# A two-layer transformer block on one NeuronCore: its feed-forward part computed with hidden units on the partitions, its expert weights loaded tile by tile

## What is computed

```
xn = layernorm(x)
x  = x + distance_attention(xn) + feed_forward(xn)       # layer 0
xn = layernorm(x)
x  = x + attention(xn) + magnitude(xn)                   # layer 1

distance_attention: 16 heads of 8; softmax(-sqrt(max(|q-k|^2, 1e-12))) @ v
feed_forward:  swiglu(h, w1, w2, w3) = (silu(h @ w1.T) * (h @ w3.T)) @ w2.T,  352 hidden units
    shared = swiglu(x, sw1, sw2, sw3)
    each token also goes to the one of 7 experts with the highest sigmoid(x @ router)
    0.5/total * shared + p/total * swiglu(x, expert's weights)
```

## Time and profile before

| | |
|---|---|
| Timed runs | median 1478.41 us (1476.91 to 1479.61, three runs) |
| Profiled execution | span 1475.7 us, first to last instruction; no other time is given for it |
| ACT busy | 1445.4 us, 98% |
| DVE busy | 1245.1 us, 84% |
| PE busy | 1125.2 us, 76%, mean granted clock 0.935 of 2.4 GHz |
| POOL busy | 632.5 us, 43% |
| DMA | 112.73 MB, 76 GB/s in the mean |

### The profile page before, as it was taken

How to read it: one execution, slowest core, us unless ns; L and a number is a source line. 1 busy time by engine, 2 the same in 40 slices (tenths; PEclk the granted TensorE clock), 3 DMA queues, 4 the chain that set the end, 5 groups by cost and what they waited for, 6 DMA issues and landing times.

```text
span 1475.7 us, 21637 instructions
## 1 busy us (share of the span) xinstructions
PE 1125.2 (76%) x7910; PEld 441.5 (30%) x7910; DVE 1245.1 (84%) x2236; ACT 1445.4 (98%) x796; POOL 632.5 (43%) x529
## 2 busy tenths in 40 slices
PE   5587786887887988878878774787778677776766
PEld 2122223144252441542524411232123122221212
DVE  6998887988989879789798787858898898998886
ACT  3999999999999999999999999999999999999998
POOL 5166460754509577595585820732113023022100
PEclk8599998999999999999999997899999999999999
DMA  4843544213242212122121321034033033021020
GB/s 124 247 137 74 160 128 124 58 52 85 79 136 65 56 43 58 38 56 64 31 66 48 84 68 31 20 108 93 28 117 76 31 110 82 27 106 34 22 72 19
DMA packets 104061, 112.73 MB, mean 76 GB/s; under 512 B 41722, under 2 KB 76026, under 8 KB 103946
## 3 DMA queue, kind: packets, MB, share of 16 engines
q1 hardware_dynamic: 98618, 99.47, 24.5%
q0 software_dynamic: 4464, 11.09, 2.7%
q10 hardware_dynamic: 864, 0.69, 0.2%
HBM read 66.52 MB, written 44.70 MB: 75 GB/s over the span
## 4 chain that ended last, share of the span: by engine, by line
ACT 72%; issue 12%; DVE 11%; PE 3%; POOL 2%; DMA 1%; SPq 0%; ACTq 0%; DVEq 0%; POOLq 0%
ACT scores L785 28%; ACT scores L746 25%; ACT exp L1304 11%; DVE exp L1312 5%; DVE scores L695 4%; ACT exp L1300 2%; ACT ht L1037 1%; ACT L785 1%; ACT L746 1%; POOL yro L1091 1%; PE pvb L676 1%; PE ring L661 1%; ACT scores L778 0%; PE ring L1279 0%; POOL at L1254 0%
## 5 line engine op out<-in xcount | busy, mean ns | idle before, releaser
L695 DVE TENSOR_SCALAR scores<-ring 128x1024 f32<-128x1024 f32 x512 | 589.7, 1216 | 28.7 <-PE ring L661 23.5
L785 ACT ACTIVATE scores<-scores 128x8192 f32<-128x8192 f32 x63 | 438.9, 7020 | 0.2
L1304 ACT ACTIVATE exp<-ring 128x1024 f32<-128x1024 f32 x438 | 432.7, 1419 | 0.2
L746 ACT ACTIVATE scores<-scores 128x8192 f32<-128x8192 f32 (+1 forms) x59 | 404.2, 6919 | 0.2
L1279 PE MATMUL ring<-stk 128*128 128x512 bf16 x1024 | 306.7, 385 | 122.8 <-ACT exp L1304 100.1
L676 PE MATMUL pvb<-scores,val 128*9 128x256 f32 x4096 | 324.6, 392 | 80.6 <-issue 38.4
L1312 DVE SCALAR_TENSOR_TENSOR exp<-exp 128x512 f32<-128x512 f32 x438 | 322.6, 758 | 62.2 <-ACT exp L1304 56.3
L661 PE MATMUL ring<-stk 64*128 64x512 bf16 x1024 | 210.4, 408 | 56.6 <-DVE scores L695 44.5
L1279 PEld LDWEIGHTS ring<-stk 128*128 128x128 bf16 x1024 | 65.8, 97 | 338.3 <-ACT exp L1304 234.4
L661 PEld LDWEIGHTS ring<-stk 64*128 64x128 bf16 x1024 | 49.9, 93 | 288.5 <-DVE scores L695 201.8
L676 PEld LDWEIGHTS pvb<-scores,val 128*9 128x9 f32 x4096 | 65.6, 89 | 210.8 <-issue 207.4
(11 more groups left out here) (263 smaller groups left out, 1415.8 us busy)
## 6 DMA issues: line engine op xcount, KB each, us to landing
stk<-stack SPq DMA_DIRECT2D x192, 192.0 KB, 2.8
stack<-qp SPq DMA_DIRECT2D x7, 768.0 KB, 4.7
stack<-kp SPq DMA_DIRECT2D x7, 768.0 KB, 5.7
xj<-xg SPq DMA_DIRECT2D x10, 448.0 KB
yg<-xj POOLq DMA_DIRECT2D x10, 448.0 KB
stack<-qp SPq DMA_DIRECT2D x7, 512.0 KB, 5.1
stack<-kp SPq DMA_DIRECT2D x7, 512.0 KB, 5.1
stk<-sum_rows SPq DMA_DIRECT2D x128, 24.0 KB
```

The costliest lines, as they stand in the source:

```text
L695: nc.vector.tensor_scalar(S[place][:, j * N:(j + 1) * N], tile, 1e-12, None, ALU.max).then_inc(o.release(("qk", group, place, j)), 1)
L746: nc.scalar.activation(part, part, ACT.Sqrt).then_inc(root_done, 1)
L785: nc.scalar.activation(S[place][:], S[place][:], ACT.Exp, scale=-1.0).then_inc(exp_done, 1)
L1304: nc.scalar.activation(EX[k // 2][:, k % 2, :], tile, ACT.Exp, scale=SCALE1).then_inc(o.release(("qk1", n, i)), 1)
```

## The change

The hidden units are put on the partitions from the start: in the up product the weights are now the stationary operand and the turned tokens the moving one, six products of 128 units x 128 tokens a tile (chunks that begin at unit 0, 128 and 224, so the last two overlap; `w2` is laid out with zeros for the repeated units). Its result can be used as stationary operand of the down product as it stands. `pe_hidden` and `dve_keep_hidden` are gone, `gate` and `h1` have 3 x 128 columns a tile instead of 352, and POOL forms (tanh + 1) * gate instead of tanh * gate + gate.

The weight buffers have seven slots, one for each tile of a round, slot 0 also for the shared weights. SP reads each routed tile's expert number into a register and loads that expert's weights into the tile's slot: 38 loads of 352 KB (up) and 38 of 192 KB (down) in place of two large ones. Those of round 7 are issued at the end of round 6; those of a later round r at its four places, up weights of round r and down weights of round r-1, two tiles of each a place, one of each at place 3. PE waits in `pe_up` and `pe_down` until all of them have landed, and reads no expert numbers any more.

```diff
+        def load_up_weights(sp, o, v, jobs):
+            if v == ROUTED_JOBS:
+                sp.wait_ge(routed, 1)
+                sp.wait_ge(placed, 16 * TOK)
+            else:
+                o.filled(sp, ("up", v - 1, JOBS - 1))
+            for j in jobs:
+                if is_routed(v, j):
+                    sp.dma_start(w13[:, j:j + 1, :, :], d["w13"][bass.ds(expert_of(sp, v, j), 1)]
+                                 .rearrange("e c a i -> c e a i")).then_inc(up_in, 16)
+
+        def load_down_weights(sp, o, v, jobs):
+            if v == ROUTED_JOBS:
+                sp.wait_ge(routed, 1)
+            else:
+                o.filled(sp, ("down", v - 1))
...
-        def pe_up(pe, o, v, e):
+        def pe_up(pe, o, v):
...
-            if v == ROUTED_JOBS:
-                pe.wait_ge(w_rest, 32)
+            if v >= ROUTED_JOBS:
+                pe.wait_ge(up_in, 16 * routed_before(v + 1))
             for j in range(JOBS):
                 tile = o.begin(pe, ("up", v, j))
                 for side in range(2):
-                    mm = nc.tensor.matmul(tile[:, side * 512:side * 512 + I], xjt[:, j * P:(j + 1) * P],
-                                          weights_of(w13, e[j])[:, :, side, :].rearrange("p o i -> p (o i)"),
-                                          start=True, stop=True)
+                    for c, first in enumerate(UNIT_CHUNKS):
+                        at_col = side * 512 + c * P
+                        mm = nc.tensor.matmul(tile[:, at_col:at_col + P], w13[:, slot_of(v, j), side, first:first + P],
+                                              xjt[:, j * P:(j + 1) * P], start=True, stop=True)
                 mm.then_inc(ring_full, 1)
...
+        def pe_down(pe, o, v):
+            tile = o.begin(pe, ("down", v))
             pe.wait_ge(hid_done, v - FIRST_JOBS + 1)
...
+            if v >= ROUTED_JOBS:
+                pe.wait_ge(down_in, 16 * routed_before(v + 1))
             for j in range(JOBS):
                 for c in range(3):
...
+                    mm = nc.tensor.matmul(tile[:, j * P:(j + 1) * P], gate[:, j, c * P:(c + 1) * P],
+                                          w2[:, slot_of(v, j), c, :], start=(c == 0), stop=(c == 2))
             mm.then_inc(ring_full, 1)
...
         def act_tanh(act, o, v):
             o.emptied(act, ("up", v, JOBS - 1))
-            nc.scalar.activation(h1, h1, ACT.Tanh, scale=0.5).then_inc(tanh_done, 1)
+            nc.scalar.activation(h1[:, :, :], h1[:, :, :], ACT.Tanh, scale=0.5).then_inc(tanh_done, 1)
...
+                        if ROUTED_JOBS < r <= LAST_JOBS + 1:
+                            jobs = range(2 * place, min(2 * place + 2, JOBS))
+                            if r <= LAST_JOBS:
+                                load_up_weights(sp, o, r, jobs)
+                            if r > ROUTED_JOBS + 1:
+                                load_down_weights(sp, o, r - 1, jobs)
                         if place == 1:
                             if FIRST_JOBS < r <= LAST_JOBS:
                                 load_jobs(sp, o, r, r - 1 - FIRST_JOBS)
```

More of the change, by code:

```diff
@@ L971, in load_jobs @@
                          ).then_inc(xj_in, 16)
[L973 to L980, removed]
         def pe_tokens(pe, o, v):
@@ L1041, in pool_hidden @@
             pool.wait_ge(tanh_done, n)
-            nc.gpsimd.tensor_tensor(h1, h1, gate[:, :, :], ALU.mult).then_inc(part_done, 1)
+            nc.gpsimd.tensor_scalar(h1[:, :, :], h1[:, :, :], 1.0, 1.0, ALU.add, ALU.mult).then_inc(part_done, 1)
             pool.wait_ge(part_done, n)
-            nc.gpsimd.tensor_tensor(gate[:, :, :], gate[:, :, :], h1, ALU.add).then_inc(hid_done, 1)
-        def dve_keep_hidden(dve, o, v, i):
-            tile = o.filled(dve, ("hidden", v, i))
-            pair = slice(2 * i, min(2 * i + 2, JOBS))
-            nc.vector.tensor_copy(ht[:, pair, :], tile.rearrange("p (j w) -> p j w", w=512)[:, 0:pair.stop - pair.start, 0:3 * P]
-                                  ).then_inc(o.release(("hidden", v, i)), 1)
+            nc.gpsimd.tensor_tensor(gate[:, :, :], gate[:, :, :], h1[:, :, :], ALU.mult).then_inc(hid_done, 1)
         def dve_keep_down(dve, o, v):
@@ L1642, in general @@
                 pe_rank(pe, o)
-                pe.wait_ge(routed, 1)
                 for v in range(FIRST_JOBS, LAST_JOBS + 1):
-                    e = [expert_of(pe, v, j) for j in range(JOBS)]
                     pe_tokens(pe, o, v)
-                    pe_up(pe, o, v, e)
-                    for i in range(PAIRS_OF_JOBS):
-                        pe_hidden(pe, o, v, i)
-                    pe_down(pe, o, v, e)
+                    pe_up(pe, o, v)
+                    pe_down(pe, o, v)
                 for b in range(B):
@@ L1690, in fast @@
                         pe_route0(pe, o, r + 1)
-                    if FIRST_JOBS < r <= LAST_JOBS + 1:
-                        for i in range(PAIRS_OF_JOBS):
-                            pe_hidden(pe, o, r - 1, i)
                     if FIRST_JOBS <= r <= LAST_JOBS:
@@ L2209, in general @@
                     dve_keep_up(dve, o, v)
-                    for i in range(PAIRS_OF_JOBS):
-                        dve_keep_hidden(dve, o, v, i)
                     dve_keep_down(dve, o, v)
@@ L2246, in fast @@
                             dve_clip(dve, o)
-                    if FIRST_JOBS < r <= LAST_JOBS + 1:
-                        for i in range(PAIRS_OF_JOBS):
-                            dve_keep_hidden(dve, o, r - 1, i)
                     if FIRST_JOBS <= r <= LAST_JOBS:
@@ L2341 @@
     w13 = np.stack([w1, w3], axis=1).transpose(0, 3, 1, 2)
-    w2c = np.zeros((NE, 3 * P, D), np.float32)
-    w2c[:, :I] = w2.transpose(0, 2, 1)
-    w2c = w2c.reshape(NE, 3, P, D).transpose(0, 2, 1, 3)
+    w2c = np.zeros((NE, P, 3, D), np.float32)
+    w2_rows, seen = w2.transpose(0, 2, 1), 0
+    for c, first in enumerate(UNIT_CHUNKS):
+        w2c[:, seen - first:, c] = w2_rows[:, seen:first + P]
+        seen = first + P
     blk = np.zeros((P, 64), np.float32)
```

81 lines of the change are left out of this document (35 added, 46 removed).

## The result

The changed kernel takes 1481.83 us (median of 8 runs, 1479.57 to 1482.67), the kernel before 1478.1 on the same chip (8 runs, 1476.62 to 1479.77): ratio 1.0026, 95% interval 1.0015 to 1.0036. It is 3.7 us slower, a quarter of a per cent; 1480.3 was predicted, within a range of 1478 to 1489. A second sample (11 runs) gave 1.0024, 1.0015 to 1.0033. The profiled run of the changed kernel took 1481.77 us, so 1.7 us lie outside its span.

A forecast was written before the change was run, and what follows sets the result against it. ACT, busy 98% of the span, was taken to bound the kernel from 40 us on. Span 1475.7 + 1.87 for the tanh = 1477.6, plus 2.7 outside it: 1480.3 us, +0.13%; range 1478 to 1489.

The forecast's parts named there:

- the one certain term: ACT's tanh, ten times: 2,688 instead of 2,464 elements a partition, 0.187 us more each, 1.87 us, all on the path.
- The feed-forward rounds with weights: PE's block in rounds 9 to 12: 20.3 against 19.5 us, 0.25 us a round carried; ACT does not wait.
- the granted clock below 1.00 in the down part: PE's down part: 4.0 us at half rate lose 2.0 us; ends: nothing, or 4.95.
- The slower rival (late weights): PE's first down matmul, rounds 9 to 12: weights land late, 1487 with 5.7 us to landing; late or cold weights 0.22.
- the lead of the fourth root: Where ACT would be hit, waiting for DVE scores in rounds 10 to 13, once 4.7 us have been carried.
- POOL and DVE: POOL 1 us longer, DVE's up part 0.7 us longer a round at most, four copies fewer: no effect on the time.
- a lead of 4.7 us, the smallest of the four places: Round 10, place 3: DVE ends its tiles at 651.5, ACT's fourth root begins at 656.2.
- from 40 us on the time is the sum of ACT's instructions: The bound: ACT busy 98%; an edit counts only if it changes its instructions or makes it wait.
- a gain of 0.5 that nothing can use: PE's block in rounds 4 to 8, down weights early: 18.95 us, 0.5 less than before, without effect on the time.
- The change does not touch that code: The start, in the faster rival: removing its largest wait, 5.2 us, would give 1475.1; chance of faster 0.05.
- The constant: 2.7 us added to the forecast span, as the median of timed runs lay that far above the profiled span.

The follow-up runs named there:

- the short tanh: The changed kernel with the tanh over 352 of the 384 columns of each tile: 1479.29 us, ratio 1.0017.
- the tokens first: Batch 1's tokens stored and batch 2's loaded before the clearing in round 0: changed kernel 1479.84 us, ratio 1.0020; kernel before 1477.24 us, 1.0002.

## Why the prediction was right, and where not

- **The tanh**, "the one certain term": 1.87 forecast, 24.3 - 22.4 = 1.9 measured in ACT's list, and about 1.5 behind 300 us, of which the short tanh gave back 1.3.
- **The feed-forward rounds with weights**: right, and nearly in every size. Last down tile 7.1 forecast, 6.9 (SP's two register loads there took 0.45 and 0.27 us, where 0.53 each had been taken); PE's wait 1.4, 1.3 on average; down part 6.95, 6.3 to 7.8 (7.04 in round 9); up part 9.9, 9.54; block 20.3, 19.7. ACT did not wait, and loads a step earlier changed nothing.
- **The clock**: "the granted clock below 1.00 in the down part": 0.68 over its 7 us, so 4.5 us of it at the lower level (1.2 GHz), and 1.00 in the up part. Before the transposes were gone it had been 1.00 there. The Trainium skill (TensorE: Matmul & The Clock Gate, Part 4: PE-mode transpose), by which the removed transposes had warmed nothing, would have left the down part at 4.95 us. The trace disagrees again: 7.04, of which the wait for weights ahead of it may explain a part, and 5.3 to 6.5 in rounds 4 to 8 (5.60 in round 6, from 418.05 us), where PE did not wait. This is weaker evidence than the earlier trace rows, for the down part now also begins sooner after PE's idle time, 3.25 us after the output turn began in round 9 instead of 6.25.
- **The slower rival (late weights)**: its price and its carrying hold, 11.7 worked out and 12.0 us of waits seen when the loads are made 5 us late. That they lie so close is in part luck, since PE's wait rose by 3.9 us a round in rounds 9 to 12 and not by the 4.8 that went into the sum. And the instruction that is hit was another: the prediction asked for the lead of the fourth root, and the tanh, at the end of the block itself, is hit before it.
- **POOL and DVE**: nothing, as forecast. POOL's two instructions take 2.42 and 5.93 us (5.96 each was the bound).
- **What failed: "a lead of 4.7 us, the smallest of the four places".** That was read in round 10 and taken for all rounds. At place 2 of round 1 it is 1.2 us in the kernel before (DVE ends at 111.8, the root comes at 113.0), and at place 3 of round 4 it is 0.3 (296.7 and 297.0); in the second profile of the same kernel ACT already waits there. A list of waits, on which "from 40 us on the time is the sum of ACT's instructions" rested, shows only leads that are already used up; a lead of 0.3 stands in no row of it. DVE's last two tiles of the two places, and ACT's roots of the two rounds (the last of each is the one meant), in the kernel before:

```profile
109.43 2.35 DVE L695 TENSOR_SCALAR scores<-ring 128x1024 f32<-128x1024 f32 x2
294.31 2.35 DVE L695 TENSOR_SCALAR scores<-ring 128x1024 f32<-128x1024 f32 x2
...
99.06 20.87 ACT L746 ACTIVATE scores<-scores 128x8192 f32<-128x8192 f32 x3
276.22 27.80 ACT L746 ACTIVATE scores<-scores 128x8192 f32<-128x8192 f32 x4
```

- **What followed from it**: round 3's block was never priced. The text has rounds 4 to 8 ("a gain of 0.5 that nothing can use") and 9 to 12, but in round 3 the longer up part has no removed transposes to set against it. It costs 1.2 to 1.3 us at the last root of round 4, the larger miss. The size of that part was known, 9.9 against 8.45 us; what was wrong was to price it only where the removed transposes paid for it.
- **"The change does not touch that code"** (on the start): true of the code, not of the addresses. A dropped tile moved the zeros, the DMA burst of round 0 lasted longer, and DVE's jump took longer. Done alone in the kernel before, this costs 1.9 us; in the changed kernel it is put at 0.7 to 0.9 from a few profiles, which does not stand clear of their scatter.
- **The constant**: the 2.7 us between the profiled span and the median were 1.7 outside the span, and 1.0 by which that profile was faster than the median. So the forecast of the span, 1477.6, was 2.5 too low (1480.1), and 1.0 of it was hidden by this term. The time came out 1.5 us above the forecast, just on the other side of the 0.2% that it had set as "no change". That it came so near is in part luck: two costs were left out, and this term covered one microsecond of them.

The round-3 cost is read from rows of pairs of kernels; no run changed that block alone. The parts do not simply add: tanh 1.87, round 3 1.2 and the moved tile alone 1.9 make 5.0, against 3.2 to 3.7 measured. ACT's waits in rounds 1, 2 and 4 can stand in for each other (where it waited 2.2 us in round 1 it waited nothing in round 4), but how much each takes from the others is not settled. Why one of SP's last two DMA issues before its branch took 0.92 to 1.57 us in all eight profiles of changed kernels, and at most 0.35 in the six of the kernel before, also stayed open; the length of the program that SP skips does not explain it.

## What to carry to other kernels

An engine that is busy 98% with an empty list of waits may still have next to no lead in some round: read the lead over it (when its input is ready, when it is wanted) in each kind of round, first and transitional ones above all, before calling an added microsecond hidden. Price a change in the rounds that get its cost without its gain, here the one round with an up part and no transposes. And when a tile goes or comes, look at what moves behind it: compare the rate of the large DMAs that read or write there, and keep the old alignment with a pad, which here brought the rate back, though its gain in time was not shown.

## What was not expected of the hardware

- A DMA that reads 1 KB a partition from a tile that begins at a multiple of 256 bytes ran, with its neighbours, at 373 to 393 GB/s while the burst lasted; from an odd multiple of 128 mostly at 340 to 385, with dips to 246 (with the tokens first, 360 to 389). The instructions were the same, and the tile was moved there in the one kernel and back in the other. Only three addresses were tried. The Trainium skill (DMA: Bandwidth & Descriptors, How a descriptor splits into AXI transactions) has the rule that fits: a descriptor is fetched in pieces of 256 bytes that begin at multiples of 256, so the first piece of one that begins elsewhere starts at the multiple below and brings bytes that are not used. By that rule, as an estimate, 1 KB from an odd multiple of 128 takes five pieces in place of four. The rates here agree with it in direction; no run counted the pieces.
- DVE's jump into another part of its program took 4.3 to 4.9 us from the branch to the first instruction behind it, and 5.7 to 6.2 when the DMA engines were busy longer. The stall has no name in the list of waits but "issue"; a packet on an instruction queue 2 us before its end gives it away. The Trainium skill (Runtime: NRT & Kernel Launch, Instruction fetch mechanics) says that a taken branch out of the stretch already fetched makes the engine wait until a DMA has brought the target. The packets here agree; that the packet comes later while other transfers keep the DMA engines busy (3.3 to 4.0 us after the branch instead of 2.1 to 2.7) is what the traces add.
